# x rows of the hop groups in three buffers, and half of the product stores issued from ScalarE's queue

## The reference

```python
pos_emb = rpe[hops]                              # hops: 512 x 512 indices, rpe: 2017 rows of 512
qh = layernorm(x)                                # split in 8 heads of 64
pe = pos_emb.reshape(Sq, Sq, NH, DH)
k_hop = jnp.einsum('bhvc,vmhc->bhvm', qh, pe)    # for each query position v its own 512 x 64 matrix
qk = jnp.einsum('bhsd,bhtd->bhst', qh, k_scaled)
C = (qk + k_hop) * D                             # D is zero for m > v
```

## Time and profile before

| | us |
|---|---|
| median of 3 runs | 3920.59 |
| lowest and highest | 3919.91 and 3928.87 |
| the profiled execution | 3928.23 |
| its span, first to last instruction | 3926.5 |

### The profile page before, as it was taken

How to read it: one execution, slowest core, us unless ns; L and a number is a source line. 1 busy time by engine, 2 the same in 40 slices (tenths; PEclk the granted TensorE clock), 3 DMA queues, 4 the chain that set the end, 5 groups by cost and what they waited for, 6 DMA issues and landing times.

```text
span 3926.5 us, 70398 instructions
## 1 busy us (share of the span) xinstructions
PE 3251.9 (83%) x24884; PEld 1936.4 (49%) x24884; DVE 2642.9 (67%) x5498; ACT 1759.0 (45%) x4225; POOL 2034.6 (52%) x2247
## 2 busy tenths in 40 slices
PE   4666666677777777589999999999999999999997
PEld 3444444454444444345555555555555555555554
DVE  5444444455455545478788888888888888888885
ACT  2333333344444444344445444554545545455442
POOL 4666666667777776134444444444444444444443
PEclk7888878888888898799999999999999999999999
DMA  7888888889999999454454555554555546555451
GB/s 229 285 281 279 283 283 295 285 283 324 320 322 325 312 315 321 138 162 137 138 168 138 145 161 157 154 152 140 171 157 155 152 140 170 157 157 150 138 156 59
DMA packets 409679, 814.14 MB, mean 207 GB/s; under 512 B 100314, under 2 KB 204762, under 8 KB 407284
## 3 DMA queue, kind: packets, MB, share of 16 engines
q1 hardware_dynamic: 322292, 524.36, 43.1%
q0 software_dynamic: 87040, 285.28, 22.8%
HBM read 632.67 MB, written 176.69 MB: 206 GB/s over the span
## 4 chain that ended last, share of the span: by engine, by line
PE 39%; DVE 21%; DMA 18%; SPq 7%; issue 6%; ACT 6%; POOL 3%; DVEq 0%; ACTq 0%
PE psum L1248 9%; DMA arena<-in_x_dram 8%; PE psum L1385 7%; PE psum L1264 5%; DMA arena<-hop_products 5%; DMA arena<-in_L_xattn_rpe_dram,arena 4%; DVE arena L1057 4%; PE psum L1336 4%; SPq L545 3%; PE psum L1328 3%; PE psum L1306 3%; PE psum L1352 3%; POOL arena L677 3%; SPq L584 2%; PE psum L1275 2%
## 5 line engine op out<-in xcount | busy, mean ns | idle before, releaser
L1248 PE MATMUL psum<-arena 128*128 128x128 f32 x4352 | 688.5, 313 | 333.0 <-ACT arena L505 124.8
L677 POOL DMA_INDIRECT arena<-in_L_xattn_rpe_dram,arena x768 | 729.5, 950 | 291.7 <-issue 182.3
L1248 PEld LDWEIGHTS psum<-arena 128*128 128x128 f32 x4352 | 566.3, 161 | 550.4 <-issue 353.1
L695 POOL TENSOR_SCALAR_AFFINE_SELECT arena<-arena 128x256 f32<-128x256 f32 x256 | 105.2, 411 | 817.8 <-ACT arena L810 685.0
L1385 PE MATMUL psum<-arena 128*128 128x512 f32 x1024 | 487.8, 605 | 29.1 <-ACT arena L795 29.1
L810 ACT ACTIVATE arena<-arena 128x512 f32<-128x512 f32 (+3 forms) x1024 | 502.6, 558 | 4.0 <-DMA arena<-gate_rows 3.9
L1057 DVE TENSOR_TENSOR arena<-psum,arena 128x1024 f32<-128x1024 f32 (+1 forms) x384 | 397.6, 1041 | 115.7 <-PE psum L1336 114.6
L1264 PE MATMUL psum<-arena 64*32 64x416 f32 (+7 forms) x8192 | 361.9, 424 | 120.5 <-ACT arena L743 50.7
L508 DVE COPY arena<-psum 128x512 f32<-128x512 f32 x384 | 265.5, 692 | 271.0 <-PE psum L1248 267.1
L668 POOL DMA_INDIRECT arena<-in_L_xattn_rpe_dram,arena x320 | 304.1, 950 | 238.9 <-PE psum L1248 132.2
L517 DVE COPY arena<-psum 128x416 f32<-128x416 f32 (+15 forms) x512 | 224.6, 442 | 271.8 <-PE psum L1264 267.7
(11 more groups left out here) (103 smaller groups left out, 4814.7 us busy)
## 6 DMA issues: line engine op xcount, KB each, us to landing
arena<-in_x_dram SPq DMA_DIRECT2D x256, 256.0 KB, 3.7
arena<-gate_rows SPq DMA_DIRECT2D x128, 512.0 KB, 4.5
arena<-in_x_dram SPq DMA_DIRECT2D x512, 64.0 KB
arena<-in_ctx_dram SPq DMA_DIRECT2D x32, 1024.0 KB, 7.9
out_dram<-arena SPq DMA_DIRECT2D x128, 256.0 KB, 2.5
arena<-in_L_xattn_rpe_dram,arena POOLq DMA_INDIRECT x1088
hop_products<-arena SPq DMA_DIRECT2D x16, 1024.0 KB
arena<-hop_products SPq DMA_DIRECT2D x128, 128.0 KB, 3.2
```

The source lines that it names most:

```text
L677: nc.gpsimd.indirect_dma_start(out=rows[v][:, t, :], out_offset=None, in_=rpe[:, :], in_offset=bass.IndirectOffsetOnAxis(ap=here[:, t, v:v ...
L1248: last = nc.tensor.transpose(turn_bank(o)[:, q * P:(q + 1) * P], own[:, q * P:(q + 1) * P], ident)
```

## The change

Three things change in the hop stage.

1. There are three `x_group` buffers (`X_BUFS = 3`). SP fills all three at the start. In the loop, SP now waits at group n for the normalization of group n+1 (which DVE does within group n, before product 0) and then loads x of group n+4 into that buffer; at group 0 it also loads that of group 3.
2. The load stands ahead of the store of group n on SP and behind that of group n-1.
3. ACT's half of the products is stored by ACT itself, at the end of its own work for the group, behind a wait for its own last product copy. SP stores DVE's half.

```diff
--- before.py
+++ after.py
@@ -113,6 +113,7 @@
 
 
     QUARTERS = 4
+    X_BUFS = 3
     DIAG = P // QUARTERS
     BODIES = SEG_GROUPS // QUARTERS
     FG = 32
@@ -169,7 +170,7 @@
 
 
         hopsT = place(ST * S).rearrange("p (t v) -> p t v", t=ST)
-        x_group = [place(DIM) for _ in range(2)]
+        x_group = [place(DIM) for _ in range(X_BUFS)]
         x_norm = place(DIM)
         x_stats = place(8)
         q_turned = [place(KT * VG * B) for _ in range(2)]
@@ -242,7 +243,7 @@
         pe_setup = sem("pe_setup")
         setup_evac = sem("setup_evac")
 
-        x_group_loaded = [sem(f"x_group_loaded{i}") for i in range(2)]
+        x_group_loaded = [sem(f"x_group_loaded{i}") for i in range(X_BUFS)]
         hop_stored = [sem(f"hop_stored{c}") for c in range(QUARTERS)]
         dve_q = Stage(sem("dve_q"), ["stats", "mean", "norm"])
         pe_q = Stage(sem("pe_q"), ["turn"])
@@ -540,24 +541,24 @@
                              (base_b_all, base_b.partition_broadcast(P))):
                 sp.dma_start(dst, src).then_inc(mgates_loaded, 16)
 
-            def load_group(par, g):
+            def load_group(n):
                 for v in range(VG):
-                    sp.dma_start(x_group[par][v * B:(v + 1) * B, :], x_groups[g, v, :, :]).then_inc(
-                        x_group_loaded[par], 16)
-
-            load_group(0, rows_of(0))
-            load_group(1, rows_of(1))
+                    sp.dma_start(x_group[n % X_BUFS][v * B:(v + 1) * B, :], x_groups[rows_of(n), v, :, :]).then_inc(
+                        x_group_loaded[n % X_BUFS], 16)
+
+            for n in range(X_BUFS):
+                load_group(n)
             sp.wait_ge(setup_evac, len(jobs))
 
             for n in range(GROUPS):
                 s, c, k = GROUP[n]
                 width = VG * hop_width(n)
-                if n + 2 < GROUPS:
-                    sp.wait_ge(dve_q.sem, dve_q.done(n, "norm"))
-                    load_group(n % 2, rows_of(n + 2))
-
-                sp.wait_ge(*act_h.at(("prod", n, VG - 1)))
-                sp.dma_start(hop_store[s][c][0, k, :, :], hop_out[c][:, 0:width]).then_inc(hop_stored[c], 16)
+
+                for m in (0, 1) if n == 0 else (n + 1,):
+                    if m + X_BUFS < GROUPS:
+                        sp.wait_ge(dve_q.sem, dve_q.done(m, "norm"))
+                        load_group(m + X_BUFS)
+
                 sp.wait_ge(*dve_h.at(("prod", n, VG - 1)))
                 sp.dma_start(hop_store[s][c][1, k, :, :], hop_out[c][:, width:2 * width]).then_inc(hop_stored[c], 16)
 
@@ -776,6 +777,10 @@
                         turned((n + 1) % 2, n + 1)
                     if evacuated_by(o, 1):
                         hop_copy(act, nc.scalar.copy, act_h, o, 1)
+
+                s, c, k = GROUP[n]
+                act.wait_ge(*act_h.at(("prod", n, VG - 1)))
+                act.dma_start(hop_store[s][c][0, k, :, :], hop_out[c][:, 0:VG * hop_width(n)]).then_inc(hop_stored[c], 16)
 
             hops_over(act)
 
@@ -953,29 +958,28 @@
             for s in TWO_TILES[1]:
                 diag_list(s)
 
-            def query_stats(par, g, half):
-
-                dve.wait_ge(x_group_loaded[par], half * 64 + 64)
-                nc.vector.bn_stats(x_stats[:, 0:6], x_group[par]).then_inc(dve_q.sem, dve_q.step("stats"))
+            def query_stats(g):
+                dve.wait_ge(x_group_loaded[g % X_BUFS], g // X_BUFS * 64 + 64)
+                nc.vector.bn_stats(x_stats[:, 0:6], x_group[g % X_BUFS]).then_inc(dve_q.sem, dve_q.step("stats"))
                 dve.wait_ge(dve_q.sem, dve_q.done(g, "stats"))
                 nc.vector.bn_aggr(x_stats[:, 6:8], x_stats[:, 0:6]).then_inc(dve_q.sem, dve_q.step("mean"))
 
-            def query_norm(par, g):
+            def query_norm(g):
                 dve.wait_ge(act_q.sem, act_q.done(g, "rstd"))
                 dve.wait_ge(pe_q.sem, pe_q.done(g, "turn", 1))
-                nc.vector.tensor_scalar(x_norm, x_group[par], x_stats[:, 6:7], x_stats[:, 7:8], ALU.subtract,
+                nc.vector.tensor_scalar(x_norm, x_group[g % X_BUFS], x_stats[:, 6:7], x_stats[:, 7:8], ALU.subtract,
                                         ALU.mult).then_inc(dve_q.sem, dve_q.step("norm"))
 
-            query_stats(0, 0, 0)
-            query_norm(0, 0)
+            query_stats(0)
+            query_norm(0)
 
             for n in range(GROUPS):
                 more = n + 1 < GROUPS
                 if more:
-                    query_stats((n + 1) % 2, n + 1, (n + 1) // 2)
+                    query_stats(n + 1)
                 for o in hop_order(n):
                     if o == ("prod", n, 0) and more:
-                        query_norm((n + 1) % 2, n + 1)
+                        query_norm(n + 1)
                     if evacuated_by(o, 0):
                         hop_copy(dve, nc.vector.tensor_copy, dve_h, o, 0)
```

## The result

| | before | changed |
|---|---|---|
| median, us | 3924.73 (4 runs) | 3837.10 (4 runs) |
| lowest and highest | 3919.91 and 3936.89 | 3833.68 and 3839.88 |
| span of the profiled execution | 3926.5 | 3834.1 |

The ratio is 0.9772, with a 95% interval of 0.9746 to 0.9797: 88 us less. 3822 had been forecast, within 3765 to 3892.

A forecast was written before the change was run, and what follows sets the result against it. POOL's gathers (85 us a turn) plus its idle time behind PE, late because of x, bound the first half; DMA was nearly saturated in the second. 82 + 16 = 98 us off the 3920.59 us median gave 3822 us, range 3765 to 3892.

The forecast's parts named there:

- The long stall: POOL's wait before the diagonal gathers (L668): 15.8 us a turn of eight groups, 7.5 left, 8.3 won.
- PE's way: The long stall ended by PE's transposes, which continue earlier without the x wait: 6.6 to 8.9 us left.
- The gathers' way: The long stall ended through the last row gather's landing, 9.28 us at longest: 0 to 8.3 us left.
- The short stall: POOL's wait before L677, on PE after another x wait: 2.3 us a turn, 0.3 left, 2.0 won.
- First half: Hop stage, first half: 8 x (8.3 + 2.0) = 82 us won, bounds 32 and 145.
- Second half: Hop stage, second half: 16 us won, between 0 and 39, as another data wait replaces the x wait on saturated engines.
- ACT's store: 128 store issues on ACT, 0.345 us each at the median, fit its 0.95 us idle gap: cost 0.
- sign of being right: Hop stage: x waits near zero, first-half turn about 93 us, L668 stall 6 to 9, DMA share 0.94 or more.
- signs of being wrong: Hop stage: PE's row waits replace x waits, landings over 12 us, ACT issues over 1 us, second half longer.
- The floor: Rival, hop stage: gathers land well under 9 us, POOL never waits, 184 us go: 3737 us; chance 0.13.
- The waits did move to the gathers: Rival, hop stage: x waits return as waits for gathered rows, only 32 us won: 3889 us; chance 0.15.
- The third queue: Rival, hop stage: stores on two queues cut the gathers' DMA share, 108 us lost: slower, 3996 us; chance 0.07.

The follow-up runs named there:

- act_only_2: Kernel before with only ACT's half of the stores moved to ACT's queue, two x buffers and late load kept: 3930.38 us, 1.0001 of the kernel before.
- x3_sp_2: Changed kernel with both stores back on SP, three x buffers and early load kept: 3828.24 us, 0.9746 of the kernel before.
- x2_early: Changed kernel with two x buffers instead of three: 0.982 and 0.9821 of the kernel before, both on chips of the second kind.
- after_2: The changed kernel measured again, unaltered, beside the kernel before on a chip as the first: 3835.50 us, 0.9757.
- diag4: Changed kernel with four buffers of diagonal tiles instead of two: 0.9895 of the kernel before on a second-kind chip; 3782.36 us, 0.963 on one as the first.

## Why the prediction was right, step by step

**The direction and the place.** As forecast, most of the gain is POOL's idle time in the first half, not DVE's 246 us of waits. `act_only_2` and `x3_sp_2` show that the buffers and the loads' place are the cause; that the place alone does it is shown on the second kind of chip only (`x2_early`).

**The long stall.** 7.5 us a turn was taken, from 15.8; 60 us in eight is 7.5. The way to it held; that it fits to a tenth is luck, since the number was picked between bounds and single stalls lie between 6.60 and 8.53. Two ways had been set against each other, PE's (6.6 to 8.9 us) and that of the last gather's landing (0 to 8.3). In the turn shown they end 0.36 us apart, and the gathers' is the later one: 7.99 us of landing and 6.5 us to POOL's release. PE's way came out near its lower end, since the transposes ran faster without the idle time ahead of them (granted clock 0.79 against 0.50), as allowed for. The gathers' way was bounded too low: the 9.28 us that the prediction took as the longest landing wasn't the longest, as the chain of before has one of 10.51 us, which would have made the end 9.5 us instead of 8.3.

**The short stall.** 0.3 was taken, 0.3 it is.

**First half.** 82 us forecast, 83.0 measured.

**Second half.** 16 us taken, between 0 and 39; 12.7 measured (95.7 less 83.0). The reason given was right: PE's wait for rows rose from 70.8 us to

```profile
PE psum L1252 <- DMA arena<-in_L_xattn_rpe_dram,arena: 118.8, 115, 4.0
```

118.8 us, and the 48 us more are two thirds of the 73.1 us that the x waits gave back. POOL's waits at L678 are 52.4 in 80, less 0.3 each is 28 us, where 39 had been, so 11 of the 12.7 us are POOL's:

```profile
POOL arena L678 <- PE psum L1252: 52.4, 80, 4.2
```

**ACT's store.** Forecast at nothing, and nothing it is, alone (1.0001) and as a part. The longest issue was 0.364 us, so that the 2.07 us of SP's queue never came up, and the 0.95 us gap hid it. ACT's idle time before L742 did not grow.

**The sum.** 98 us forecast, 95.7 at the end of the hop stage, 92.4 in the span, 88 in the medians. The last step is the spread of the runs: the profiled execution of before was 3.5 us above its median, that of the changed kernel 0.9 below, and `after_2` with its own before gave 92 us. 3837 is 15 us above the 3822 since the median of before, from which the gain was taken off, also rose, from 3920.59 to 3924.73 us with a fourth run.

**The signs.** One that was named as a sign of being right failed by a little: the DMA share of the first half is 0.93, not 0.94 or more. None of the signs of being wrong came.

**The rivals.** The floor was not reached: the distance from the last gather to POOL's release stayed. The waits did move to the gathers in part: 112.6 us from 40.9 in the first half, 72 us more where 173.0 us of x waits went. But POOL's long stalls shrank all the same, to 60 us; what the rival mispriced is that a wait of PE for rows costs nothing as long as it doesn't stop POOL. That reading fits the rows and was not tested by a run. The third queue did not make it slower. The longest landing in the chain of waits (which shows only gathers that something waited for) was 9.72 us (10.20 in `after_2`), as against 10.51 us before:

```profile
217.60 9.72 DMA arena<-in_L_xattn_rpe_dram,arena
```

```profile
441.49 10.51 DMA arena<-in_L_xattn_rpe_dram,arena
```

## What to carry to other kernels

When an engine waits long for a load, don't price the load's wait: find the engine whose idle time lengthens the turn (here the one that issues the gathers), ask what it would wait for next, and take the difference. A prefetch is as good as the time between its issue and its use, so its place in the queue, ahead of the stores of the same step, can count for more than another buffer (here shown on the second kind of chip). Where turns mix large and small steps, look at the pair with the least work between release and use: two small groups in a row needed one more buffer, and on a chip as the first it was worth 1.4%, where the change itself was worth 2.4%.

## What the runs showed of the hardware that I had not expected

- The same program took 3928 us on one chip and 4442 and 4390 us on others, with a lower DMA share (0.70 against 0.87) and ACT and DVE waiting over 400 us each for an event without an instruction in the trace; the cause is open. Gains have to be compared on one chip: four diagonal buffers had the least gain of the three kernels with an early load on the one (`diag4`, 0.9895) and the most on the other (`diag4_2`, 0.963).
- The DMA engines were held at a share of 0.99 and 338 GB/s for 340 us (`diag4_2`) with the gathers still at one in 1.25 us.
- An issue of a store of up to 1 MB on ACT's queue took 0.33 to 0.36 us each time, while on SP's queue, behind other transfers, stores had taken up to 2.07 us and x loads up to 2.2 us. In the changed kernel the median x load issue fell from 0.883 us to 0.423 us. It is the load's place and the third buffer that do it, not ACT's stores leaving SP's queue: with both stores back on SP (`x3_sp_2`) it is 0.422 us. The changed kernel:

```profile
L546 SPq DMA_DIRECT2D arena<-in_x_dram x512: 310/423/1990, 13.8 to 1430.5; - x171
```
